# Adjacency signs as bytes: two column tiles in one 16-bit word, turned at once on TensorE

## The reference, cut to what matters

```python
feat_1 = x @ a[:F];  feat_2 = x @ a[F:]            # x is layer-normalised here
e = leaky_relu(feat_1 + feat_2.T, 0.2)
U = softmax(where(adj > 0, e, NEG_INF), axis=1)     # 4096 x 4096
prop_u = U @ x; rowsum = sum(U * 0.5 * U, axis=1)   # round one
feat = soft_threshold(...)                          # of x, prop_u, rowsum
pu = U @ feat                                       # round two
x = x + out(feat, pu, h0, temp)
x = x + mamba2_block(layernorm(x))                  # runs beside round two
```

## Time and profile before

| | us |
|---|---|
| median of three runs (lowest, highest) | 868.73 (866.70, 872.04) |
| the profiled execution | 869.0 |
| its span, first to last instruction | 867.3 |
| from the start until round one's products run steadily | 79 |
| round one with turns (supertile 0 to 6) | 79 to 366 |
| supertile 7, products alone | 366 to 398 |
| round two beside the Mamba block, and the tail | 398 to 867 |

### The profile page before, as it was taken

How to read it: one execution, slowest core, us unless ns; L and a number is a source line. 1 busy time by engine, 2 the same in 40 slices (tenths; PEclk the granted TensorE clock), 3 DMA queues, 4 the chain that set the end, 5 groups by cost and what they waited for, 6 DMA issues and landing times. The chain is left out here.

```text
span 867.3 us, 22265 instructions
## 1 busy us (share of the span) xinstructions
PE 800.7 (92%) x6654; PEld 763.9 (88%) x6654; DVE 749.8 (86%) x1966; ACT 676.8 (78%) x1402; POOL 581.1 (67%) x1220
## 2 busy tenths in 40 slices
PE   3977999998999899997899999999999999999956
PEld 1667999998999899997789999999999999999945
DVE  6558899996999799988699999999999999999852
ACT  6667888876877787895588888888888898898751
POOL 4462366654666566675588887787787787788850
PEclk9689999998999999999899999999999999999975
DMA  6446979786878687622211112111111111110000
GB/s 197 135 158 188 309 228 297 241 278 201 272 243 276 231 254 261 202 98 66 62 62 65 46 57 67 39 63 60 42 63 60 42 63 60 39 43 14 8 3 10
DMA packets 97547, 110.74 MB, mean 128 GB/s; under 512 B 6464, under 2 KB 89280, under 8 KB 97472
## 3 DMA queue, kind: packets, MB, share of 16 engines
q1 hardware_dynamic: 97472, 109.74, 39.8%
HBM read 90.85 MB, written 18.87 MB: 127 GB/s over the span
## 5 line engine op out<-in xcount | busy, mean ns | idle before, releaser
L1121 ACT ACTIVATE maskA<-code 128x1024 fp32r<-128x1024 int8 x256 | 268.4, 1051 | 49.5 <-DVE code L688 26.6
L1387 PE MATMUL accA<-Y,maskA 128*128 128x260 f32 (+1 forms) x1792 | 274.7, 297 | 18.7 <-ACT maskA L1121 13.4
L1397 PE MATMUL accC<-Y,maskC 128*128 128x260 f32 (+1 forms) x1792 | 256.4, 286 | 1.8 <-DVE maskC L696 1.8
L1387 PEld LDWEIGHTS accA<-Y,maskA 128*128 128x128 f32 x1792 | 236.7, 194 | 21.7 <-ACT maskA L1121 14.2
L1397 PEld LDWEIGHTS accC<-Y,maskC 128*128 128x128 f32 x1792 | 232.7, 192 | 2.7 <-DVE maskC L696 2.7
L688 DVE SCALAR_TENSOR_TENSOR code<-f_rows,neg_f,ps 128x512 int8<-128x512 f32 x256 | 178.6, 741 | 40.7 <-PE ps L1327 39.3
L696 DVE TENSOR_SCALAR maskC<-code 128x1024 fp32r<-128x1024 int8 x256 | 212.2, 830 | 0.0
L1061 ACT ACTIVATE edges<-adj_in 128x1024 bf16<-128x1024 f32 x128 | 133.1, 1045 | 22.9 <-DMA adj_in<-in_adj_dram 17.0
L593 POOL TENSOR_TENSOR room_r<-room,room_r 128x256 fp32r<-128x256 f32 x128 | 94.3, 765 | 2.5
L1327 PE MATMUL ps<-ident,edges 128*128 128x128 bf16 x1024 | 82.2, 225 | 12.7 <-ACT edges L1061 9.2
L956 DVE SCALAR_TENSOR_TENSOR room<-room 128x128 f32<-128x128 f32 x288 | 92.2, 342 | 0.0
(11 more groups left out here) (230 smaller groups left out, 1625.4 us busy)
## 6 DMA issues: line engine op xcount, KB each, us to landing
adj_in<-in_adj_dram SPq DMA_DIRECT2D x128, 512.0 KB, 4.6
edge_codes<-code SPq DMA_DIRECT2D x8, 2048.0 KB, 9.6
code<-edge_codes SPq DMA_DIRECT2D x32, 512.0 KB, 3.3
xn<-in_x_dram SPq DMA_DIRECT2D x4, 512.0 KB, 5.6
room<-in_x_dram SPq DMA_DIRECT2D x32, 64.0 KB, 1.8
room<-in_L_gnn_h_dram SPq DMA_DIRECT2D x32, 64.0 KB, 1.9
out_dram<-room SPq DMA_DIRECT2D x32, 64.0 KB, 1.6
room<-in_L_ffn_W_in_dram SPq DMA_DIRECT2D x1, 192.0 KB, 2.7
```

Of the source, the lines that this page charges most:

```text
L1121: s.activation(maskA[:, b % MASKS], src, ACT.Relu, bias=-2.0).then_inc(S["maskA_ready"], 1)
L1387: t_.matmul(accA[k][:, 0:2 * cols], maskA[:, b % MASKS, l * P:(l + 1) * P], y2_of(jt, 0) if cols == F else Y[:, jt, 0, :, 0:cols], start=j ...
L1397: m = t_.matmul(accC[k][:, 0:2 * cols], maskC[:, b % MASKS, l * P:(l + 1) * P], y2_of(jt, 1) if cols == F else Y[:, jt, 1, :, 0:cols], sta ...
```

## The change

Three constants are new: `FREE` 2, `LINK` 127 and `HUGE` 1e30. The sign becomes Relu(1e30 * adj + 2) written as int8: 2 where there is no edge, and the largest byte, 127, where there is one. It is written at a step of two bytes, so that byte 0 of a 16-bit word is from the block's first column tile and byte 1 from its second. `edges` has the same size, now 8 slots of 4 x 128 words. TensorE reads the words as bf16 and multiplies them by the identity (no longer twice it): 4 matmuls for a block, both column tiles at once, into one bank. The upper half of each fp32 word in PSUM is the bf16 word, so VectorE reads byte 2 (first tile) or byte 3 (second) of every fourth byte. The code is (feat_1 <= -feat_2) - byte: -2 and -1 are no edges, -127 is maskA, -126 is maskC, and the masks' constants change with it. Each of the four banks now holds a block, so a turn waits for the codes of the block four earlier, and a sign for the turn eight blocks earlier.

```diff
+HUGE = 1e30
+FREE = 2.0
+LINK = 127.0
+    EDGE_SLOTS = 8
-        edges, Y2_2a = shared("edges", [P, 4, IT, 2 * P], BF16, [("Y2_2a", [P, JB, 2, F], F32R)])
+        edges, Y2_2a = shared("edges", [P, EDGE_SLOTS, IT, P], BF16, [("Y2_2a", [P, JB, 2, F], F32R)])
-            g.affine_select(out=ident2[:], in_=ident2[:], compare_op=ALU.not_equal, fill=2.0, base=0,
+            g.affine_select(out=ident2[:], in_=ident2[:], compare_op=ALU.not_equal, fill=1.0, base=0,
...
+            def turned(jt):
+                words = ps[jt // JH % TRB][:, :].bitcast(I8)
+                return words.rearrange("p (i r y) -> p i r y", i=IT, y=4)[:, :, :, 2 + jt % JH]
             def codes(G, par, jt):
...
-                    scalar=neg_f2[:, jt:jt + 1], in1=ps[jt % TRB][:, :].rearrange("p (i r) -> p i r", i=IT),
-                    op0=ALU.is_gt, op1=ALU.add).then_inc(S["coded"], 1)
+                    scalar=neg_f2[:, jt:jt + 1], in1=turned(jt),
+                    op0=ALU.is_le, op1=ALU.subtract).then_inc(S["coded"], 1)
...
-                v.tensor_scalar(maskC[:, b % MASKS], src, 2.0, None, ALU.is_equal).then_inc(S["maskC_ready"], 1)
+                v.tensor_scalar(maskC[:, b % MASKS], src, 1.0 - LINK, None, ALU.is_equal).then_inc(S["maskC_ready"], 1)
...
-                    act.wait_ge(S["tr_done"], n * 2 - 6)
-                s.activation(edges[:, h % 4], adj_in[:, h % 4], ACT.Sign).then_inc(S["signed"], 1)
+                    wait(act, "tr_done", (n - EDGE_SLOTS + 1) * JH)
+                pair = edges[:, h % EDGE_SLOTS].bitcast(I8).rearrange("p i (w e) -> p i e w", e=JH)
+                s.activation(pair, adj_in[:, h % 4].rearrange("p i (e w) -> p i e w", e=JH), ACT.Relu, bias=FREE, scale=HUGE).then_inc(S["signed"], 1)
...
-                s.activation(maskA[:, b % MASKS], src, ACT.Relu, bias=-2.0).then_inc(S["maskA_ready"], 1)
+                s.activation(maskA[:, b % MASKS], src, ACT.Relu, bias=1.0 - LINK, scale=-1.0).then_inc(S["maskA_ready"], 1)
...
                 pe.wait_ge(S["signed"], G * BLOCKS + b + 1)
-                for j in range(JH):
-                    jt = b * JH + j
-                    if not (first and jt < TRB):
-                        pe.wait_ge(S["coded"], G * NT + (jt - TRB + 1))
-                    for it in range(IT):
-                        m = t_.matmul(ps[jt % TRB][:, it * P:(it + 1) * P], edges[:, b % 4, it, j * P:(j + 1) * P], ident2[:], start=True, stop=True)
-                    m.then_inc(S["tr_done"], 1)
+                if not (first and b < TRB):
+                    pe.wait_ge(S["coded"], G * NT + (b - TRB + 1) * JH)
+                for it in range(IT):
+                    m = t_.matmul(ps[b % TRB][:, it * P:(it + 1) * P], edges[:, b % EDGE_SLOTS, it], ident2[:], start=True, stop=True)
+                m.then_inc(S["tr_done"], JH)
```

## The result

The changed kernel takes 847.2 us (846.3 to 848.3) against 870.3 in the same series: ratio 0.974, 95% interval 0.9703 to 0.9778. That is 23 us less, inside the range of 847 to 866, at its lower edge; I had forecast 14 us less, 855.

What follows compares the result with a forecast made beforehand. TensorE was taken to set round one's pace, 0.04 us a block over VectorE, which then takes over. From 869.0 us, 11.2 less in the window and 2.7 before 79 us gave 855.1, predicted as 855; range 847 to 866.

Steps and rivals of the forecast that it cites:

- VectorE's code and the sign: Round one: VectorE's code was taken at 741 ns as before, ScalarE's sign at 1045 ns with a doubling as upper bound.
- The row that I set as the upper bound: VectorE product with spaced-out operands, 0.68 us for 128 elements; at that price a code would take over 2.7 us.
- The pace: Round one: TensorE's block falls from 2.44 to 2.225 us; VectorE's 2.40 is then longest, 0.04 us a block gained.
- The idle time left to VectorE: Round-one window: 13.4 us idle on top of VectorE's 262.3 us of work, 275.7 us in all, 11.2 less.
- (a): TensorE's two jumps back: 5.8 us each before, 2.2 us absorbed at each by TensorE's lead, 7.2 us stay.
- (b): First blocks of supertile 0, where TensorE's 2.225 us still rules: about 3 us of VectorE idle, with the start.
- (c): DMA waits, half covered by TensorE's lead, and seven supertile starts at 0.45 us: 3.2 us of VectorE idle.
- Rival 2: At the jumps back, TensorE's lead of two whole blocks hides 4.8 us each instead of 2.2; 849 us, chance 0.13.
- Before 79 us: Start of the kernel: fewer turning matmuls and no sign's wait save 2.7 to 3.7 us; 2.7 taken.
- Banks: Four banks for four blocks rather than four column tiles let TensorE run further ahead of VectorE; no separate size given.
- After 366 us: Behind round one's turns: nothing changes, as the masks read bytes as before.
- The signs that I named: Expected in the profile: 512 turning matmuls about 41 us busy, maskC waits appearing, VectorE's turn waits from 39 to under 28.

Runs made afterwards that it cites:

- run 10: Changed kernel with long-satisfied waits ahead of accA's matmuls only inside TensorE's round-one loop, none ahead of or behind it; 856.8 us, ratio 0.9865.
- run 5: Changed kernel, a block's four turning matmuls move 384, 256, 256 and 128 columns instead of 128 each; 853.9 us, ratio 0.9823.
- run 6: Changed kernel with one extra long-satisfied semaphore instruction ahead of each accA matmul in round one, inside and outside the loop; 847.2 us, ratio 0.9743.
- Run 7: Changed kernel, but a sign waits for the turn four blocks earlier instead of eight; 850.0 us, ratio 0.9786.
- run 9: Kernel before, with 128 long-satisfied waits added in supertile 0, ahead of TensorE's loop; 857.9 us, ratio 0.9885.
- run 8: Changed kernel, but a turn waits for the codes of the block two earlier instead of four; 847.8 us, ratio 0.976.
- run 11: Changed kernel with VectorE's 128x2 operation q_c, the square of the row sum, moved to ScalarE; 846.8 us, ratio 0.9764.
- run 12: Kernel of run 11 with the 2 MB spill cut into four 512 KB DMAs, a load of adjacency after each; 841.1 us, ratio 0.9698.
- run 3: Changed kernel with every turning matmul issued twice; 867.7 us, ratio 0.9992.
- run 4: Changed kernel with four tiny matmuls, one column by one column, ahead of each turn; 869.5 us, ratio 1.001.

## Why the prediction was right, and where it was off

*VectorE's code and the sign.* Taken at 741 and 1045 ns, measured 740 and 1053. The row that I set as the upper bound had nothing to do with it. The rule of the Trainium skill that I weighed ("Advanced Engine Details and Errata", Memory Cachelines, on patterns in PSUM that aren't contiguous) doesn't hold for this VectorE read: a byte of every fourth costs what the whole word does. This row decides.

*The pace.* 2.225 us worked out for TensorE, 2.21 measured. That VectorE takes over was right: its busy time in the window was put at 262.3 us and is 260.6. Its own 2.40 us a block are there too. Windows of the changed kernel over the first 16 blocks and the next 16, columns as in the earlier trace rows:

```profile
75.30:117.80 42.50, 41.31 (x349) 39.88 (x350) 39.58 (x67) 35.55 (x40) 18.97 (x52) 0.94 0.81 259
117.80:156.40 38.60, 36.45 (x321) 34.51 (x320) 37.89 (x69) 31.95 (x37) 25.95 (x72) 1.00 0.84 272
```

From the second row on, 16 blocks take 38.5 to 38.9 us, 2.41 to 2.43 each.

*The idle time left to VectorE* is where the forecast missed. It was put at 13.4 us: (a) 7.2 at the two jumps, (b) and (c) 6.2 for all else. Measured: 267.0 - 260.6 = 6.4 us, and no stand at the jumps. (b) and (c) were right, and not by luck: VectorE is idle for 42.50 - 39.58 = 2.9 us in the first 16 blocks, (b) had 3, and for the other 3.5 us in the rest, (c) had 3.2. (a) was mis-sized, 7.2 us for nothing. The step that failed is the sentence by which a jump back costs TensorE the same 3.5 us and VectorE's wait is only shortened by TensorE's lead. The stand belongs to the loop's instructions, their place and their number. The change left out 128 matmuls ahead of the loop and 128 in it, each with its weight load. By the counts in the last section the loop still begins at the same place in a block of 256 (118 past a multiple, before 120), but it is shorter, 1376 instructions for 1662; run 10 begins at that place too, has 1632, and has the stand. So it is the shorter loop that lost it. Rival 2 (849) named the right size, but its mechanism, a lead of two whole blocks that hides the jump, isn't what happened: with TensorE as full as before (run 5) the jump is free too, and where the stand is there (run 10) the lead covers only part of it: VectorE waits 3.28 us at the first jump, 4.93 before. That run is the kernel which the prediction described, the change with the stands left in: 856.8 us, against the forecast 855 (its added waits cost nothing by themselves, as run 6 shows).

*Before 79 us.* 2.7 us were forecast; the second turn of supertile 1 starts at 75.30 (TensorE's timeline of after), not 79.12, 3.8 us earlier:

```profile
75.30 0.61 PE L1335 MATMUL ps<-ident,edges 128*128 128x128 bf16 x4 [5.52 <-ACT edges L1071]
```

The eight codes that had waited 1.97 us begin without a wait:

```profile
67.86 5.35 DVE L697 SCALAR_TENSOR_TENSOR code<-f_rows,neg_f,ps 128x512 int8<-128x512 f32 x8
```

Run 7 puts 2.0 us of this to the eight slots by the profiled executions (2.8 by the medians), where I had counted 1 to 2; the rest is the shorter turns, of which I had expected 1.7. Single executions scatter here by as much: in run 9, which runs the kernel of before up to there but for satisfied waits, the same turn starts at 77.0 us, not 79.1.

*Banks.* I let the four banks add to the lead; run 8 shows nothing of it.

*After 366 us.* Nothing was to change; in the two profiles the part from the last turn on takes 504.1 us after (845.6 - 341.5) and 502.0 before (867.3 - 365.3). The 2 us are within the scatter of single executions: run 5 shares this part with after, instruction for instruction, and takes 500.2 (851.7 - 351.4).

*Parts of the gain.* Taken from the ratios times 868.5 us: before to run 9 (the jumps alone) 10.0 us; run 9 to run 5 (bytes, slots and banks, TensorE's array time as before, no jump price in either) 5.4 us; run 5 to after (the array time) 7.2 us. They add up to 22.6 by the way they are made. From the intervals, the first has an uncertainty of about 3 us, the other two of about 5 each, so that the second is hardly more than its own. Two other comparisons agree: run 10 less run 6 gives 9.6 us for the stands in the changed kernel, and before less run 10 gives 11.7 us for all else. So of the 23 us, some 12.6 are the change's own work (slots, bytes, fewer columns through TensorE) and some 10 came by the stands, which went as the loop got shorter; in the kernel before, a shift of 128 instructions would have won them just as well (run 9). The forecast of 14 less counted the first and held the second to be fixed.

*The signs that I named.* 512 turns, as said; their busy time is 51 us, not 41, since the row holds the way through the array, which I had warned of for 225 ns and then forgot: four in a row overlap less than eight.

One sign didn't come: TensorE's waits for maskC, which were to appear, are 1.7 us over the whole run (1.8 before). What TensorE waits more for, now that VectorE sets the pace, are VectorE's codes, which free the banks: its weight loads for the turns wait 9.6 us for them in the window, 4.3 before.

## What to carry to other kernels

Before a forecast that goes over a hardware loop, read the page's line of instruction packets and look for a stand at the jumps: an edit that only changes the number of instructions can win or lose two stands, here 10 us, and satisfied waits ahead of the loop, here 128, show at once whether its place matters. When an engine is relieved and the next one is 0.04 us a block behind, count the floor by the next engine's work and then add its waits one by one; outside the jumps that sum was right here (6.2 us of waits forecast, 6.4 measured). And what a step takes off the new bound may be lost to the next wait in the chain (run 11), until that one is cut too (run 12).

## What the runs showed of the hardware

A taken jump back on TensorE cost 3.0 to 4.2 us of stand and then some 1.3 to 2.7 us more by the lower clock behind it, by the starts of the matmuls (the granted clock was 0.54 in those 3.6 us of run 10), or nothing. Four kernels have the stand (before and runs 3, 4 and 10, with 45 or 46 packets), eight with the loop have none (after and runs 5 to 9, 11 and 12, with 26 to 28). Runs 6 and 10 have 28 and 45 packets, and run 10's stream is one packet shorter (256 waits fewer outside the loop), so its two jumps cost 18 packets, 9 for each.

The profile of DMAs for a window shows when they come. Before, from 190 to 360 us, which is from ahead of the first jump almost to the end of the last pass, it has this line of instruction packets:

```profile
q8 instruction: 18, 0.29, 0.8%
```

After, from 185 to 354 us, which is the second and third pass and the start of supertile 7, it has no line of that queue, and only these:

```profile
q1 hardware_dynamic: 35703, 44.46, 80.0%
q14 instruction: 1, 0.01, 0.0%
```

So the changed kernel's TensorE runs the body again from what it holds, and that of before fetches all of it again in each pass.

The body's place explains both: where it begins so that it should touch 8 blocks of 256 instructions they are fetched again, where it should touch 7 they aren't. The trace shows no addresses, so the absolute place is not shown, but TensorE's instructions can be counted in it. Ahead of the loop's first pass there are 1400 (before), 1398 (runs 3 and 4) and 1142 (run 10), all 118 to 120 past a multiple of 256, and these have the stand; in runs 9 and 6 there are 1528 and 1270, 248 and 246 past one, and these have none. Shown is that moving the loop by 128 instructions turns the stand on and off, in both kernels (runs 9, 6 and 10); that the limit is 7 blocks is inferred. By that count the changed kernel's loop, 1376 instructions or 5.4 blocks, touches 6 or 7 wherever it begins.

The Trainium skill, "Runtime: NRT & Kernel Launch", Instruction fetch mechanics, gives TensorE 128 KB for instructions in blocks of 16 KB, which is 8, and says that a taken branch outside the current window of two blocks has to fetch. The runs agree with the size of the blocks (16.3 KB a packet) and fit the 8 blocks. They don't agree with a window of two on TensorE: its loops of 1376 to 1662 instructions, 5.4 to 6.5 blocks by that count, jumped back with no stand in eight kernels. Here the measurement decides.

VectorE reads one byte of each fp32 word in PSUM at the price of the word (740 ns for 128x512), and ScalarE writes bytes at a step of two at the price of bf16 (1053 ns for 128x1024).
